# Pacing the gathers of a GNN layer: a gather begins when the last but one has landed, on four semaphores in turn

## The chip, the cores and the metric

The kernel runs on one core of one Trainium2 chip. The metric is the device time in microseconds (us) of one execution, and the median of several such executions. A profiled execution has a span, which is the time from its first to its last instruction on the core, and a device time of its own beside it.

The names in the profile: PE is TensorE (its matmuls), PEld its weight loads, DVE is VectorE, ACT is ScalarE, POOL is GpSimd, SP is SyncE. A `q` behind a name (SPq, ACTq) is the engine's instruction queue, where it issues transfers. L480 is line 480 of the kernel before.

## The reference

One message-passing layer over 12,500 nodes and 412,500 edges, which are sorted by their target:

```python
edge_index = jnp.stack([src, dst])
h = jnp.maximum(_layernorm(x, axis=-1), 0.0)            # x: (12500, 32)
e_feat = jnp.concatenate([h[rol], h[col], edge_attr], axis=-1)   # rol = src, col = dst, 412500 edges
h1 = jax.nn.relu(e_feat @ W1 + b1)                      # W1: (96, 64)
v = h1 @ W2 + b2                                        # W2: (64, 32)
x_cand = jax.ops.segment_max(v, col, num_segments=num_nodes)
x = x + jnp.maximum(x_cand, h)
```

## The kernel before

**Tiles.** The edges are cut into C = 403 chunks of CE = 1024. A chunk's 1024 source rows lie in eight columns of 128. Seven of them (GK = COLS - 1 = 7) are fetched by GpSimd, one indirect DMA for a column: 128 rows of 128 bytes out of `h_rows` in device memory into `feat`. The eighth column is made on chip, by a product of one-hot keys with a table (`select` on TensorE, `take_selected` on VectorE). There are 7 x 403 = 2821 gathers in all.

**Rings.** `feat` has UNROLL = 16 slots, one chunk each, so GpSimd can be up to 16 chunks ahead of TensorE. Each slot has a semaphore of its own, `gathered0` to `gathered15`. A gather adds 16 to it when it has landed, a chunk's seven add TURN = 112. GpSimd waits at every second chunk for `feat_turned`, which says that TensorE has read the slot that is to be filled again; besides, at every eighth chunk, for the indices.

**Steps.** TensorE works in steps of two chunks (202 steps: the last has one chunk). A step v on TensorE holds, in this order: `first_layer(v-1)` (ps_hid, L580 and L582), `turn_ends(v-2)` (ps_turned, L603), `turn_features(v)` (ps_feat, L537: it waits for the gathers, transposes the chunk and raises `feat_turned`), `select` (ps_spare, L570, 14 matmuls), `second_layer(v-1)` (ps_val, L591), `pick_ends(v-2)` (ps_picked, L612), `select` again. VectorE takes each `select`'s result at L958, in the order of its own program, and then the running maximum (L929) that `turn_ends` waits for. ScalarE takes `ps_hid` at L722.

**Loads.** ScalarE's queue issues, at every second step, the target places (L255, 512 KB) and edge attributes (L258, 512 KB) of four chunks. SyncE's queue issues for the same four chunks the term rows (L320, 64 KB each), keys (L336) and keep masks (L326). All orders are written out by hand; nothing is scheduled by a planner.

**Around the loop.** Ahead of the steps stand the layer norm and the terms of each node (`node_terms`, which copies at L296 and L304 what TensorE made); behind them the final maximum.

Of the kernel before, what the change touches and what calls it, by code (L numbers as in the profile page):

```python
# [20 lines left out]
UNROLL = 2 * RING  # L21
TWO = 2
UP = UNROLL // TWO
IDX = 4 * RING
PRE = 5
GK = COLS - 1
SA = 14
SG = 7
ROUND = 1.5 * 2 ** 23
# [6 lines left out]
def gnn_layer(nc, x, src, dst, edge_attr, W1, b1, W2, b2, src_cols, dst_first, attr_rows, sel_rows, sel_cols, out):  # L36
# [23 lines left out]
    REST = N - FULLP * T  # L60
    assert FULLP < P and T == SA * SG
    CPAD = sel_rows.shape[0]
    SN = SA * D

# [9 lines left out]
    def rows_of(b):  # L74
        return min(P, C - b * P)

    ctx = ExitStack()
    with ctx:
        def sb(name, shape, dt=F32):
            return ctx.enter_context(nc.sbuf_tensor(name, shape, dt))  # L80
# [4 lines left out]
        def sem(name):  # L85
            return ctx.enter_context(nc.semaphore(name))
# [21 lines left out]
        key_i = sb("key_i", [P, SG], I32)  # L108
        off_i = sb("off_i", [P, SA], I32)
        off_place = sb("off_place", [P, SA])  # L110

# [72 lines left out]
        s_names = """const_ready root_ready blocks_ready w_in row_pad pads dst_in firsts_in x_win_in  # L184
            cent_done sq_done var_ready std_ready norm_step h_even_done h_stored
            base_step fall_done keep_staged end_staged half_ready end_turned end_kept loc_staged stage_pad zeros_ready term_stored
            chunk_begun feat_turned feat_t_ready edge_hot_ready hid_sum hid_ready val_sum val_ready
            best_half run_ready ends_turned ends_ready ends_split pick_ready best_done best_zero
            check_step worst_ready flag_turned flag_ready
            fin_turned fin_max fin_step out_ready out_done  # L190
# [1 line left out]
            any_in any_gather_begun any_turned any_t_ready any_hid_sum any_hid_ready  # L192
            any_val_sum any_val_ready any_begun any_zero any_done any_all_done"""
        S = {n: sem(n) for n in s_names.split()}
        s_gather = [sem(f"gathered{r}") for r in range(UNROLL)]
        s_idx = [sem(f"idx_in{n}") for n in range(IDX // RING)]
        s_keep = [sem(f"keep_in{n}") for n in range(2)]
        s_key = [sem(f"key_in{n}") for n in range(2)]
# [20 lines left out]
        AUX = 16 * (2 + FOUR)  # L219
        NP, NG = -(-C // TWO), -(-C // FOUR)  # L220
        LOOPS = (NP - PRE) // UP
        TURN = 16 * GK

        def known(s):
            return isinstance(s, int)
# [17 lines left out]
        def wide(i, v):  # L243

            return min(TWO, C - TWO * v) if known(i) else TWO
# [203 lines left out]
        def _(pool):  # L449
# [6 lines left out]
            nc.gpsimd.iota(key_i[:], pattern=[[1, SG]], base=0, channel_multiplier=SG).then_inc(S["const_ready"], 1)  # L456
            nc.gpsimd.iota(off_i[:], pattern=[[1, SA]], base=0, channel_multiplier=0).then_inc(S["const_ready"], 1)

            pool.wait_ge(S["blocks_ready"], 2)
            for a in range(2):  # L460
                for z, row in enumerate((0, 2 * D)):
                    k = 2 * D * z + D * a
# [9 lines left out]
            def step(i, c):  # L472
                slot = c % UNROLL
                if c % RING == 0:
                    pool.wait_ge(s_idx[c // RING % 4], i * 16 + (c // IDX * 16 + 16))
                if c % TWO == 0 and (not known(i) or c >= UNROLL):
                    pool.wait_ge(S["feat_turned"], i * UNROLL + ((c - UNROLL) // TWO + 1))
                pool.sem_inc(S["chunk_begun"], 1)
                for k in range(GK):
                    nc.gpsimd.indirect_dma_start(  # L480
                        feat[:, slot, k, :], None, h_dram,
                        bass.IndirectOffsetOnAxis(ap=idx[:, c % IDX, k:k + 1].bitcast(U32), axis=0),
                    ).then_inc(s_gather[slot], 16)

            begin = UNROLL + (C - UNROLL) % IDX
            for c in range(begin):
                step(0, c)
            with pool.Fori(0, (C - begin) // IDX) as i:
                for u in range(IDX):
                    step(i, begin + u)  # L490
# [25 lines left out]
        def _(pe):  # L516
# [12 lines left out]
            def turn_features(i, v):  # L529
                n = wide(i, v)  # L530
                pe.wait_ge(S["sel_ready"], i * UNROLL + TWO * v + n)
                for c in range(TWO * v, TWO * v + n):
                    slot = c % UNROLL
                    pe.wait_ge(s_gather[slot], i * TURN + (c // UNROLL * TURN + TURN))
                    for b in range(2):
                        to = 2 * P * (c % TWO) + P * b
                        mm = pe.transpose(ps_feat[:, to:to + P],  # L537
                                          feat[:, slot, Q * b:Q * b + Q, :].rearrange("p q d -> p (q d)"), ident[:])
                mm.then_inc(S["feat_turned"], 1)
# [4 lines left out]
            for b in range(NB):  # L544
                r = rows_of(b)
# [71 lines left out]
            def step(i, v):  # L617
                if later(i, v):
                    first_layer(i, v - 1)
                if later(i, v - 1):  # L620
                    turn_ends(i, v - 2)
                turn_features(i, v)
                if is_chunk(i, TWO * v + 2):
                    select(i, TWO * v + 2)
                if later(i, v):
                    second_layer(i, v - 1)
                if later(i, v - 1):
                    pick_ends(i, v - 2)
                if is_chunk(i, TWO * v + 3):
                    select(i, TWO * v + 3)  # L630
# [54 lines left out]
        def _(act):  # L685
            act.wait_ge(S["root_ready"], 1)
            nc.scalar.activation(root_first[:], root_first[:], ACT.Sqrt)
            for n, (a, z) in enumerate(halves):
# [6 lines left out]
            nc.scalar.copy(table[0][:].rearrange("p g (f a) -> p g a f", f=D),  # L695
                           h_even.rearrange("p (g a) f -> p g a f", a=SA)).then_inc(S["table_ready"], 1)
            act.wait_ge(S["base_step"], 3)
# [91 lines left out]
        def _(dve):  # L789
# [164 lines left out]
            def take_selected(i, c):  # L954
                if known(i) and c % TWO:
# [8 lines left out]
                dve.wait_ge(S["sel_step"], i * UNROLL + c + 1)  # L964
                nc.vector.tensor_reduce(feat[:, c % UNROLL, GK, :], sel_tmp[:].rearrange("p (f a) -> p f a", a=SA),  # L965
                                        AX.X, ALU.add).then_inc(S["sel_ready"], 1)
# [142 lines left out]
```

## Time and profile before

| | us |
|---|---|
| median of 3 executions | 4759.94 (4747.39 to 4760.97) |
| the profiled execution, device time | 4765.93 |
| the profiled execution, span | 4764.1 |
| POOL busy (2716.6 of it in 2821 gathers, 963 ns each) | 2733.4 (57%) |
| PE busy | 2960.5 (62%) |
| DVE busy | 2078.8 (44%) |
| ACT busy | 748.1 (16%) |
| mean share of the 16 DMA engines | q10 9.1%, q1 7.4%, q0 (the gathers) 7.1% |
| mean granted clock of TensorE | 0.801 of full speed |

Busy time is time in which an engine executes; a POOL gather counts as busy only while its descriptors are made, not until its rows have landed. The time in which an engine waits is ended by a releaser, which the profile infers: another engine's operation, a DMA, "issue" (nothing that it shows) or "remote" (an update of a semaphore that it can't put to an operation in time).

### The profile page before, as it was taken

To read this page: it belongs to the slowest core of one execution; us is meant where nothing else is said; L and a number is where in the kernel's file an instruction comes from. 1 tells how busy PE (TensorE), PEld (TensorE's weight loads), DVE (VectorE), ACT (ScalarE), POOL (GpSimd) and SP (SyncE) were. 2 spreads that over 40 slices of the span, in tenths; PEclk is the share of its full clock that TensorE was granted. 3 is DMA by queue.
4 is the path that set the end of the run, shared out by engine and by line. 5 is a ranking of instruction groups with operands and counts; after the bars stand their busy time and mean duration, and the time that the engine had idled before them with its cause. 6 is when DMAs were issued, how large, how long until landed. Compare 5 with 4: busy or idle time off the path is not lost.

```text
span 4764.1 us, 41821 instructions
## 1 busy us (share of the span) xinstructions
PE 2960.5 (62%) x11492; PEld 2111.3 (44%) x11492; DVE 2078.8 (44%) x3562; ACT 748.1 (16%) x1058; POOL 2733.4 (57%) x2852
## 2 busy tenths in 40 slices
PE   1266566567676666666666666565766656565677
PEld 0144344445454444444444444444544444444445
DVE  5044344444444444444444444343444434444447
ACT  3011111111111111111111111111111111111111
POOL 6456555556665556565566556555655555565550
PEclk8578778788787878887888887778878888787788
DMA  4322222222222222222222222222222222221222
GB/s 99 76 58 53 46 54 47 52 49 59 49 53 47 56 50 55 50 54 47 53 51 51 54 49 51 51 47 52 55 48 50 47 53 51 49 58 43 53 52 44
DMA packets 245595, 252.33 MB, mean 53 GB/s; under 512 B 83265, under 2 KB 199479, under 8 KB 239113
## 3 DMA queue, kind: packets, MB, share of 16 engines
q10 hardware_dynamic: 20790, 103.55, 9.1%
q1 hardware_dynamic: 133938, 101.54, 7.4%
q0 software_dynamic: 90784, 46.48, 7.1%
q14 instruction: 73, 0.59, 0.0%
q8 instruction: 10, 0.16, 0.0%
HBM read 239.86 MB, written 11.52 MB: 53 GB/s over the span
## 4 chain that ended last, share of the span: by engine, by line
another core or an unknown queue 44%; PE 21%; DVE 15%; issue 14%; DVEq 3%; ACT 3%; ACTq 1%; SPq 0%; DMA 0%; POOL 0%; POOLq 0%
PE ps_spare L570 11%; DVE sel_tmp L958 3%; DVE running L929 3%; DVE best L995 3%; PE ps_turned L603 2%; DVE key_hot L947 2%; DVEq L989 2%; PE ps_hid L582 2%; PE ps_val L591 1%; PE ps_feat L537 1%; PE ps_hid L580 1%; DVE edge_hot L940 1%; PE ps_picked L612 1%; DVE feat L965 1%
## 5 line engine op out<-in xcount | busy, mean ns | idle before, releaser
L480 POOL DMA_INDIRECT feat<-h_rows,idx x2821 | 2716.6, 963 | 1900.3 <-issue 993.3
L570 PE MATMUL ps_spare<-table,key_hot 128*128 128x448 f32 x5642 | 1500.6, 426 | 395.6 <-DVE sel_tmp L958 348.0
L570 PEld LDWEIGHTS ps_spare<-table,key_hot 128*128 128x128 f32 x5642 | 1259.8, 230 | 524.3 <-DVE sel_tmp L958 339.0
L958 DVE SCALAR_TENSOR_TENSOR sel_tmp<-off_place,offset,ps_spare 128x448 f32<-128x448 f32 x403 | 273.6, 679 | 1553.4 <-remote 1234.1
L603 PE MATMUL ps_turned<-ident,running 128*128 128x128 f32 x806 | 171.9, 351 | 939.4 <-DVE running L929 733.7
L722 ACT ACTIVATE hidden<-ps_hid,b_col 128x1024 f32<-128x1024 f32 x202 | 224.8, 1113 | 2681.5 <-remote 2196.6
L603 PEld LDWEIGHTS ps_turned<-ident,running 128*128 128x128 f32 x806 | 116.2, 175 | 1088.5 <-DVE running L929 805.1
L980 DVE TENSOR_TENSOR ends<-ps_turned,ends 128x512 fp32r<-128x512 f32 x202 | 139.5, 690 | 786.4 <-ACT ends L734 579.8
L995 DVE TENSOR_TENSOR best<-ps_picked,best 32x64 f32 x1612 | 355.0, 220 | 162.9 <-remote 96.6
L947 DVE TENSOR_TENSOR key_hot<-dst_rows,ps_iota 128x1792 fp32r<-128x1792 f32 x202 | 406.1, 2011 | 18.1 <-DMA dst_rows<-key_rows 18.1
L580 PE MATMUL ps_hid<-feat_t,w_blk 128*128 128x512 f32 x806 | 413.8, 595 | 0.0
L582 PE MATMUL ps_hid<-edge_hot,term_ring 128*128 128x512 f32 x806 | 411.5, 592 | 0.0
L612 PEld LDWEIGHTS ps_picked<-end_hot,ends 128*128 128x128 f32 x1612 | 238.6, 219 | 296.7 <-issue 157.2
L612 PE MATMUL ps_picked<-end_hot,ends 128*128 128x256 f32 x1612 | 284.1, 326 | 108.5 <-DVE ends L980 63.2
L591 PE MATMUL ps_val<-hidden,w_blk 128*64 128x512 f32 (+1 forms) x808 | 240.5, 676 | 176.8 <-ACT hidden L722 113.3
L741 ACT COPY feat_t<-ps_feat 64x512 f32<-64x512 f32 x404 | 234.3, 580 | 207.0 <-remote 145.1
L965 DVE TENSOR_REDUCE feat<-sel_tmp 128x32 f32<-128x448 f32 x403 | 249.9, 620 | 13.9
L929 DVE TENSOR_TENSOR_SCAN running<-dst_rows,ps_val 128x512 f32<-128x512 bf16 x202 | 243.9, 1207 | 0.0
L971 DVE TENSOR_TENSOR end_hot<-ps_iota,end_all 128x1024 fp32r<-128x1024 f32 x202 | 241.5, 1195 | 0.0
L582 PEld LDWEIGHTS ps_hid<-edge_hot,term_ring 128*128 128x128 f32 x806 | 152.8, 190 | 194.2 <-issue 194.2
L750 ACT ACTIVATE ps_val<-ps_val,b_col 128x512 f32<-128x512 f32 x202 | 133.5, 661 | 614.8 <-PE ps_val L591 304.4
L580 PEld LDWEIGHTS ps_hid<-feat_t,w_blk 128*128 128x128 f32 x806 | 155.5, 193 | 103.5 <-issue 96.2
(125 smaller groups left out, 893.7 us busy)
## 6 DMA issues: line engine op xcount, KB each, us to landing
dst_rows<-loc_rows ACTq DMA_DIRECT2D x98, 512.0 KB
feat_t<-attr_rows_in ACTq DMA_DIRECT2D x98, 512.0 KB
feat<-h_rows,idx POOLq DMA_INDIRECT x2821
dst_rows<-key_rows SPq DMA_DIRECT2D x101, 256.0 KB
term_ring<-term_rows SPq DMA_DIRECT2D x404, 64.0 KB
dst_rows<-keep_rows SPq DMA_DIRECT2D x100, 256.0 KB
term_rows<-best SPq DMA_DIRECT2D x3, 1792.0 KB
idx<-src_cols_in SPq DMA_DIRECT2D x51, 32.0 KB
```

The lines of the kernel that those rows point to most:

```text
L480: nc.gpsimd.indirect_dma_start(feat[:, slot, k, :], None, h_dram, bass.IndirectOffsetOnAxis(ap=idx[:, c % IDX, k:k + 1].bitcast(U32), axis=0),
L570: mm = pe.matmul(ps_sel, key_hot[:, c // TWO % 2, g, P * (c % TWO):P * (c % TWO) + P], table[half][:, g, :], start=(g == 0 and half == 0), ...
L580: pe.matmul(ps_hid[:, c, :], w1_blk[:], feat_t[:, slot, :], start=True, stop=False, skip_group_check=True)
L582: mm = pe.matmul(ps_hid[:, c, :], term_ring[:, slot, :], edge_hot[:, c, :], start=False, stop=True, skip_group_check=True)
L591: mm = pe.matmul(ps_val[HID * r:HID * r + HID, 0:n * 2 * P], w2_blk[:], hidden[:, 0:n, r, :], start=True, stop=True, skip_group_check=True)
L603: mm = pe.transpose(ps_turned[:, to:to + P], running[:, c, b, :], ident[:])
L612: mm = pe.matmul(ps_picked[:, Q * WIN * c:Q * WIN * c + Q * WIN], ends[half][:, c, b, :], end_hot[:, c, Q * b:Q * b + Q, :].rearrange("p q ...
L929: nc.vector.tensor_tensor_scan(running[:, 0:n, :, :].rearrange("p c b n -> p (c b n)"), keep_ring[:, slot:slot + n, :].rearrange("p c n -> ...
L947: nc.vector.tensor_tensor(key_hot[:, v % 2, :, :], key_ring[:, slot:slot + TWO, :].rearrange("p c e -> p (c e)").unsqueeze(1) .broadcast_t ...
L958: nc.vector.scalar_tensor_tensor(out=sel_tmp[:].rearrange("p (f a) -> p f a", a=SA), in0=off_place[:].unsqueeze(1).broadcast_to([P, D, SA] ...
L965: nc.vector.tensor_reduce(feat[:, c % UNROLL, GK, :], sel_tmp[:].rearrange("p (f a) -> p f a", a=SA), AX.X, ALU.add).then_inc(S["sel_ready ...
L995: mm = nc.vector.tensor_tensor(col, ps_picked[D * q:D * q + D, to:to + WIN], col, ALU.max)
```

## The change

Every gather from the third on first waits on GpSimd until the gather two before it has landed, and counts this in a new semaphore `paced`, on which nobody waits. The 16 semaphores of the slots give way to four, which take the gathers in turn: gather number `at` uses `gathered[at % 4]`. TensorE, which waited for a chunk on one semaphore, now waits on all four.

```diff
+LANES = 4
+NEAR = 2
...
-            chunk_begun feat_turned feat_t_ready edge_hot_ready hid_sum hid_ready val_sum val_ready
+            chunk_begun paced feat_turned feat_t_ready edge_hot_ready hid_sum hid_ready val_sum val_ready
...
-        s_gather = [sem(f"gathered{r}") for r in range(UNROLL)]
+        s_gather = [sem(f"gathered{r}") for r in range(LANES)]
...
-        TURN = 16 * GK
+        TURN = 16 // LANES * GK
...
                 for k in range(GK):
+                    at = GK * c + k
+                    if at >= NEAR:
+                        pool.wait_ge(s_gather[(at - NEAR) % LANES],
+                                     i * (IDX * TURN) + 16 * ((at - NEAR) // LANES + 1))
+                        pool.sem_inc(S["paced"], 1)
                     nc.gpsimd.indirect_dma_start(
                         feat[:, slot, k, :], None, h_dram,
                         bass.IndirectOffsetOnAxis(ap=idx[:, c % IDX, k:k + 1].bitcast(U32), axis=0),
-                    ).then_inc(s_gather[slot], 16)
+                    ).then_inc(s_gather[at % LANES], 16)
...
                     slot = c % UNROLL
-                    pe.wait_ge(s_gather[slot], i * TURN + (c // UNROLL * TURN + TURN))
+                    for at in range(GK * c + GK - LANES, GK * c + GK):
+                        pe.wait_ge(s_gather[at % LANES], i * (UNROLL * TURN) + 16 * (at // LANES + 1))
```

On GpSimd (POOL), before, two chunks in the middle of the loop: one wait ahead of 14 gathers (x13 stands for 13 rows alike).

```order
L477 REGISTER_ALU
L480 DMA feat<-h_rows,idx 128x32 [waits feat_turned]
L480 DMA feat<-h_rows,idx 128x32 x13
```

The same place after the change (L487 is the gather, L484 the wait on a lane, L479 the wait for `feat_turned`): the first gathers of two chunks.

```order
L479 ISA
L487 DMA feat<-h_rows,idx 128x32 [waits feat_turned,gathered2]
L487 DMA feat<-h_rows,idx 128x32 [waits gathered3]
L484 REGISTER_ALU
L487 DMA feat<-h_rows,idx 128x32 [waits gathered0]
L487 DMA feat<-h_rows,idx 128x32 [waits gathered1]
L487 DMA feat<-h_rows,idx 128x32 [waits gathered2]
L487 DMA feat<-h_rows,idx 128x32 [waits gathered3]
```

Each gather has a wait of its own now, and at every fourth stands a register operation more, for the value that the next round waits for.

On TensorE (PE), before, `turn_features` of a step near the program's start: a wait on one semaphore for each chunk.

```order
L537 MATMUL ps_feat<-ident,feat 128x128 [waits gathered4,sel_ready]
L537 MATMUL ps_feat<-ident,feat 128x128
L537 MATMUL ps_feat<-ident,feat 128x128 [waits gathered5]
L537 MATMUL ps_feat<-ident,feat 128x128
```

The same rows after the change (L545).

```order
L545 MATMUL ps_feat<-ident,feat 128x128 [waits gathered3,gathered2,gathered0,gathered1,sel_ready]
L545 MATMUL ps_feat<-ident,feat 128x128
L545 MATMUL ps_feat<-ident,feat 128x128 [waits gathered2,gathered3,gathered1,gathered0]
L545 MATMUL ps_feat<-ident,feat 128x128
```

The matmuls are the same and stand in the same order; three waits more stand ahead of each chunk.

## Rows read from the trace of the kernel before

**Rows 1.** The page: the span, the chain that ended last, the gathers' group
```profile
span 4764.1 us, 41821 instructions
...
another core or an unknown queue 44%; PE 21%; DVE 15%; issue 14%; DVEq 3%; ACT 3%; ACTq 1%; SPq 0%; DMA 0%; POOL 0%; POOLq 0%
...
L480 POOL DMA_INDIRECT feat<-h_rows,idx x2821 | 2716.6, 963 | 1900.3 <-issue 993.3
```

**Rows 2.** Windows of the whole run: busy us of each engine (instructions), granted clock, DMA share, GB/s
```profile
0.00:232.00 232.00, 46.10 (x143) 28.86 (x144) 81.09 (x108) 51.23 (x49) 125.95 (x138) 0.69 0.36 88
232.00:4627.00 4395.00, 2803.11 (x10826) 2004.63 (x10825) 1900.08 (x3279) 668.26 (x966) 2599.96 (x2709) 0.80 0.23 51
4627.00:4714.00 87.00, 86.30 (x394) 59.70 (x392) 68.38 (x119) 25.24 (x38) 0.00 (x0) 1.00 0.23 54
4714.00:4764.10 50.10, 25.05 (x136) 18.12 (x132) 29.28 (x57) 3.37 (x7) 7.51 (x5) 0.73 0.21 33
```

**Rows 3.** Waits of POOL: us in total, times, longest
```profile
POOL feat L480 <- PE ps_feat L537: 626.6, 82, 16.4
```

**Rows 4.** Timeline of one step: start us, us, operation [idle before <-releaser]
```profile
2017.32 1.19 POOL L480 DMA_INDIRECT feat<-h_rows,idx  x1 [8.65 <-PE ps_feat L537]
2018.81 0.95 POOL L480 DMA_INDIRECT feat<-h_rows,idx  x1 [0.30 <-issue]
...
2023.07 3.01 PE L570 MATMUL ps_spare<-table,key_hot 128*128 128x448 f32 x14
...
2033.01 0.68 DVE L958 SCALAR_TENSOR_TENSOR sel_tmp<-off_place,offset,ps_spare 128x448 f32<-128x448 f32 x1 [6.62 <-remote]
...
2033.82 0.95 POOL L480 DMA_INDIRECT feat<-h_rows,idx  x1 [0.30 <-issue]
...
2036.43 1.06 PE L537 MATMUL ps_feat<-ident,feat 128*128 128x128 f32 x4
...
2038.28 0.95 POOL L480 DMA_INDIRECT feat<-h_rows,idx  x1 [3.51 <-PE ps_feat L537]
```

**Rows 5.** Timeline of a step behind the last gather
```profile
4629.81 0.60 PE L537 MATMUL ps_feat<-ident,feat 128*128 128x128 f32 x4
...
4635.24 3.05 PE L570 MATMUL ps_spare<-table,key_hot 128*128 128x448 f32 x14
...
4638.56 0.68 DVE L958 SCALAR_TENSOR_TENSOR sel_tmp<-off_place,offset,ps_spare 128x448 f32<-128x448 f32 x1
...
4642.00 0.60 PE L537 MATMUL ps_feat<-ident,feat 128*128 128x128 f32 x4
```

**Rows 6.** Timeline of ACT ahead of the steps (the node terms)
```profile
151.67 0.27 ACT L296 COPY running<-ps_val 128x128 f32<-128x128 f32 x1 [16.26 <-remote]
...
168.47 0.27 ACT L296 COPY running<-ps_val 128x128 f32<-128x128 f32 x1 [16.26 <-remote]
...
198.66 0.27 ACT L296 COPY running<-ps_val 128x128 f32<-128x128 f32 x1 [1.59 <-PE ps_val L526]
```

**Rows 7.** Windows behind a run of gathers, without loads (columns of Rows 2)
```profile
2035.60:2035.80 0.20, 0.20 (x2) 0.20 (x3) 0.20 (x1) 0.00 (x0) 0.00 (x0) 0.50 0.29 36
2035.80:2036.00 0.20, 0.20 (x2) 0.20 (x2) 0.20 (x1) 0.00 (x0) 0.00 (x0) 0.50 0.01 0
```

**Rows 8.** Timeline: two issues of ACT's load, and the last gather ahead of a pause
```profile
1990.67 0.58 ACTq L255 DMA_DIRECT2D dst_rows<-loc_rows  x1
...
2007.72 0.95 POOL L480 DMA_INDIRECT feat<-h_rows,idx  x1 [0.30 <-issue]
...
2037.32 0.58 ACTq L255 DMA_DIRECT2D dst_rows<-loc_rows  x1
```

**Rows 9.** Windows in and behind the stretch of that load (columns of Rows 2)
```profile
2005.00:2007.00 2.00, 0.00 (x0) 0.00 (x0) 0.00 (x0) 0.00 (x0) 1.48 (x2) 0.87 0.19 60
...
2012.00:2013.00 1.00, 0.00 (x0) 0.00 (x0) 0.92 (x2) 0.97 (x1) 0.00 (x0) 0.50 0.12 31
...
2014.00:2016.00 2.00, 1.44 (x7) 1.44 (x8) 1.62 (x2) 0.28 (x1) 0.00 (x0) 0.50 0.00 0
```

## The prediction

> **What bounds the kernel now.** I read the page first, because its chain says whether an engine is the bound. It isn't: 44% of the 4764.1 us, some 2096 us, lie with "another core or an unknown queue", no engine has more than 21%, and the gathers' group has 1900.3 us of idle time before it [rows 1]. So I cut the run into windows [rows 2]. Between 232 and 4627 us GpSimd issues 2709 gathers, 14 to a step, so 193.5 steps take 4395 us: 22.7 us a step and 1.62 us a gather. Behind the last gather, from 4627 to 4714 us, TensorE is busy for 86.30 of 87.00 us, and the step is over in 12.19 us (from L537 at 4629.81 to L537 at 4642.00) [rows 5], though the DMA engines' share is 0.23 in both windows. Loads alone don't slow a step; gathers do.
>
> The timeline of one step shows how [rows 4]. GpSimd is 16 chunks ahead and full; it waits for `feat_turned` (626.6 us of such waits are put to TensorE [rows 3]), then issues 14 gathers, each 0.95 us and 0.30 us behind the one before, 17.5 us in all. L570 ends at 2023.07 + 3.01 = 2026.08, yet VectorE, which waits for it, starts L958 at 2033.01, 6.93 us late. Behind the last gather the same pair is 0.27 us apart (4638.29 to 4638.56) [rows 5]. Ahead of the steps it is the same: ScalarE's copies of TensorE's results come every 16.80 us while gathers run and wait 16.26 us, and wait 1.59 us when they have stopped [rows 6]. So TensorE's results are announced late while gathers run in a row, GpSimd then pauses, since it is full, and the pause lets them through. A step is 17.5 us of gathers and a pause, 8.65 and 3.51 us in these rows.
>
> **The change part by part.** The loads, the matmuls and the gathers stay. What moves is when a gather starts. Its start becomes the landing of the gather two before it, plus the time from a semaphore to a gather's start. That time is now hidden, since the queue is fed ahead, except at a burst's start: L537 ends at 2036.43 + 1.06 = 2037.49, and the gather starts at 2038.28, 0.79 us later [rows 4]. It contains a wait and an increment already, so `paced` is costed at nothing more; if every wait cost another 0.30 us, the gap between gathers, each gather would.
>
> *Landing, quiet.* No row shows a landing. The last gather of a burst starts at 2033.82, and the share of the DMA engines is 0.29 until 2035.8 and 0.01 after [rows 4, 7]: 2.0 us. A gather that starts behind a wait takes up to 1.19 instead of 0.95 us [rows 4]. I take 2.2. Two gathers to 2.2 + 0.79 us is 1.50 us each, against 1.25.
>
> *Landing beside the loads.* ScalarE's load comes every 2037.32 - 1990.67 = 46.65 us, for four chunks, 28 gathers [rows 8], and its engines are busy until the window of 2014, so for some 23 us [rows 9]. The landing there is 2.2 at least and, since the gather of 2007.72 had surely landed by 2014.0, 6.3 us at most. I take 3.5, nearer to the low end, because the engines' mean share is only 0.19 there [rows 9] and two gathers are under way instead of 6.3 / 1.25 = 5. That is (3.5 + 0.79) / 2 = 2.15 us a gather.
>
> *Sum.* Of 28 gathers 23 / 2.15 = 10.7 begin beside the loads, the other 17.3 take 17.3 x 1.50 = 26 us: 49 us for four chunks, against 45.4 now. GpSimd becomes the bound: 24.5 us for 14 gathers. Under it lie TensorE's 12.19 us a step and even its late announcements. The first 112 gathers fill the ring by 30 + 112 x 1.50 = 198 us, ahead of the 232 us at which the first slot is free again. Then 2709 / 28 = 96.75 groups x 48.95 = 4736 us, and behind them a landing of 2.2 and the 50.1 us of the last window [rows 2], as TensorE is no longer behind: 232 + 4736 + 52 = 5020 us of span. The profiled execution's own time is 1.8 us above its span and 6.0 above the median: 5016 us, 5.4% slower.
>
> TensorE's three waits more for each chunk, six a step, have no row; at the 0.30 us of a GpSimd gap they are 1.8 us a step. I take nothing: TensorE would have 24.5 us for 12.19. If GpSimd weren't the bound, they could cost 193.5 x 1.8 = 350 us.
>
> The notes on the chip speak of the same landing. The Trainium skill, "DMA: Bandwidth & Descriptors", in "Anatomy of one DMA — SWDGE (gpsimd) path", gives a DMA from GpSimd a fixed 2.0 us, mostly the receipt of the last write, plus bytes / 436e3: an estimate of 2.04 us for 16 KB. The quiet windows agree (2.0 us). By that figure for all gathers, also beside loads, the interval would be 1.42 us and the sum 4127 us.
>
> **The rivals.** *Faster: the landing stays short beside the loads.* The same sum with 1.50 us for all 2709 gathers is 232 + 4064 + 52 = 4348 of span, 4344 us. For it speak the low share of the engines and the prompt step behind the last gather [rows 5, 9]. Against it: loads of 1 MB are issued at once, and the burst's last gather may take 6.3 us. It decides at one number: four chunks must take under (4764 - 284) / 96.75 = 46.3 us, so 12.5 gathers must fit in 23 us, 1.84 us each, a landing of 2.89 us. The fixed cost that the Trainium skill states as constant is this case. The same page, in "Queues, rings and completion order", says that each DMA engine takes turns between its queues a packet at a time, which would lengthen it; no row here separates the queues. Chance 0.21.
>
> *Much slower.* Either the landing beside loads is near 6.3 us: 3.55 us a gather, 6.5 in 23 us and 21.5 x 1.50 = 32.3 behind: 55.3 us for four chunks, 5630 us. Or the slower flow still holds back TensorE's announcements until GpSimd pauses: a step is then 24.5 us and a pause of 3.51, 28.0, and 193.5 x 28.0 + 284 - 4 = 5698 us. Ahead of the steps the gathers did it without the steps' loads [rows 6]; no row shows them at 1.50 us. Chance 0.24.
>
> *Nothing changes.* If the queue hides the 0.79 us, a landing of 2.2 us is over before the gather two later would start anyway (2.5 us), and beside loads 1.75 us a gather still gives 13.1 in 23 us and 14.9 x 1.25 = 18.6 behind, 41.6 in all, under the 45.4 of now. The steps and their pauses stay: 4760 us. Against it stands that the wait comes ahead of the issue, where the 0.79 us was measured. Chance 0.07.
>
> **How the numbers follow.** The forecast, 4800 to 5250 us, has 0.48. A measurement of this kernel tells about 0.3% from no change, 14 us. Faster: 0.21 and a little of the third: 0.22. Within: 0.05. Slower: 0.73. For 8 in 10 I leave out the ends of both rivals, a tenth at each side: 4480 to 5560; the forecast's own range is 4800 to 5250, for landings beside loads of 3.0 to 4.4 us and 0.03 us more or less in quiet time.
>
> **What the profile would show.** Right: GpSimd's gathers mostly wait on a DMA or "remote" and not on TensorE; their starts lie 1.5 us apart in quiet time and about 2 beside loads; the wait for `feat_turned` is gone; TensorE's idle time is ended by gathers at `turn_features`; the end comes some 52 us behind the last gather. L958 follows L570 within a microsecond more often than now. Wrong: intervals under 1.65 us on the mean (faster), or waits for `feat_turned` that stay beside late L958s (the announcements are still held back). I'd be wrong above all by the landing beside loads, which no row gives.

## The result, and the profile after

The changed kernel takes 6042.69 us (median of 4 executions, 6032.24 to 6050.42), the kernel before beside it 4753.66 (4 executions, 4707.94 to 4760.97): a ratio of 1.274, interval 1.265 to 1.282. It is slower, as forecast, but by 27% and not by 5.4%, and it lies outside the range. The profiled execution took 6032.24 us.

The page of the changed kernel: its span, the chain that ended last, and the groups of the gathers and of `turn_features`.

```profile
span 6030.4 us, 46408 instructions
...
DMA 60%; issue 26%; POOL 12%; POOLq 1%; DVE 1%; PE 0%; DVEq 0%; SPq 0%; ACT 0%
...
L487 POOL DMA_INDIRECT feat<-h_rows,idx x2821 | 2701.2, 958 | 3269.4 <-DMA feat<-h_rows,idx 2342.8
L545 PE MATMUL ps_feat<-ident,feat 128*128 128x128 f32 x806 | 211.2, 355 | 2992.7 <-DMA feat<-h_rows,idx 2991.1
```

Before, 44% of the chain lay with "another core or an unknown queue" [rows 1]. Now 60% is the landing of gathers and 12% their making. A gather is still made in 958 ns; the idle time before gathers has grown from 1900.3 us [rows 1] to 3269.4, and landings end most of it (2342.8 us). TensorE waits for gathers, 2991.1 us in all.

The waits of the changed kernel: us in total, times, longest.

```profile
DVE sel_tmp L966 <- PE ps_spare L578: 3474.1, 199, 25.5
...
PE ps_feat L545 <- DMA feat<-h_rows,idx: 2991.1, 220, 22.6
...
POOL feat L487 <- DMA feat<-h_rows,idx: 2342.8, 1192, 7.4
...
POOL feat L487 <- issue: 907.3, 1628, 7.3
```

No wait of GpSimd is put to TensorE any more (626.6 us before [rows 3]): its ring is never full. VectorE's wait at L966 is now ended by TensorE itself; none of its waits ends in "remote", as this one did before:

```profile
DVE sel_tmp L958 <- remote: 1234.1, 156, 27.8
```

GpSimd's timeline around one load of ScalarE in the changed kernel.

```profile
3022.41 0.95 POOL L487 DMA_INDIRECT feat<-h_rows,idx  x1 [1.40 <-DMA feat<-h_rows,idx]
3023.66 0.95 POOL L487 DMA_INDIRECT feat<-h_rows,idx  x1 [0.30 <-issue]
3025.49 1.32 POOL L487 DMA_INDIRECT feat<-h_rows,idx  x1 [0.89 <-issue]
3031.30 0.95 POOL L487 DMA_INDIRECT feat<-h_rows,idx  x1 [4.48 <-DMA feat<-h_rows,idx]
3033.17 0.95 POOL L487 DMA_INDIRECT feat<-h_rows,idx  x1 [0.93 <-DMA feat<-h_rows,idx]
3037.30 0.95 POOL L487 DMA_INDIRECT feat<-h_rows,idx  x1 [3.18 <-DMA feat<-h_rows,idx]
3038.98 0.95 POOL L487 DMA_INDIRECT feat<-h_rows,idx  x1 [0.73 <-DMA feat<-h_rows,idx]
3044.31 0.95 POOL L487 DMA_INDIRECT feat<-h_rows,idx  x1 [4.38 <-DMA feat<-h_rows,idx]
...
3056.81 0.95 POOL L487 DMA_INDIRECT feat<-h_rows,idx  x1 [0.85 <-DMA feat<-h_rows,idx]
...
3063.09 0.95 POOL L487 DMA_INDIRECT feat<-h_rows,idx  x1 [4.01 <-DMA feat<-h_rows,idx]
3064.34 0.95 POOL L487 DMA_INDIRECT feat<-h_rows,idx  x1 [0.30 <-issue]
3066.31 0.95 POOL L487 DMA_INDIRECT feat<-h_rows,idx  x1 [1.03 <-DMA feat<-h_rows,idx]
3067.57 0.95 POOL L487 DMA_INDIRECT feat<-h_rows,idx  x1 [0.30 <-issue]
3069.53 0.95 POOL L487 DMA_INDIRECT feat<-h_rows,idx  x1 [1.02 <-DMA feat<-h_rows,idx]
```

From its timeline of all engines: one `select` and VectorE behind it, and the issues of loads.

```profile
3016.78 3.05 PE L578 MATMUL ps_spare<-table,key_hot 128*128 128x448 f32 x14
...
3020.10 0.68 DVE L966 SCALAR_TENSOR_TENSOR sel_tmp<-off_place,offset,ps_spare 128x448 f32<-128x448 f32 x1
...
3023.44 0.58 ACTq L257 DMA_DIRECT2D dst_rows<-loc_rows  x1
...
3056.67 0.59 SPq L328 DMA_DIRECT2D dst_rows<-keep_rows  x1
```

If a gather starts 0.79 us [rows 4] behind the landing of the one two before it, starts give landings (the time from a gather's start to its landing). Quiet: 3069.53 - 0.79 - 3066.31 = 2.43 us, and a pair every 3.22 us, 1.61 us a gather. Beside the load: 3031.30 - 0.79 - 3023.66 = 6.85 us, 3037.30 - 0.79 - 3031.30 = 5.21, 3044.31 - 0.79 - 3037.30 = 6.22, and for the gather of 3033.17, which is waited for by that of 3038.98, 5.02: 5.0 to 6.9 us. Seven intervals take 3044.31 - 3022.41 = 21.9 us, 3.13 us a gather. A second disturbance of 5.49 us (3063.09 - 0.79 - 3056.81) stands beside SyncE's load of keep masks at 3056.67. L578 ends at 3019.83, and L966 starts 0.27 us later, so this result is prompt; that of rows 4 was taken 6.93 us late.

This stretch isn't a rare one. Between 1500 and 4500 us the trace has 51 whole rounds of four chunks from one issue of ScalarE's load to the next, 58.8 us each. On the mean the gathers that start within 21 us of the issue take 22.1 us for 6.9 intervals, 10.9 us more than 6.9 x 1.61; the other 21 of a round take 2.8 us more than at 1.61. SyncE issues its four term rows in the same 21 us (in the round of 3023.44 from 3024.41 to 3041.09).

The same windows of the changed kernel: first behind the load's issue, then the remainder of its stretch, then a quiet one (columns of Rows 2).

```profile
3027.00:3029.00 2.00, 0.00 (x0) 0.00 (x0) 0.00 (x0) 0.00 (x0) 0.00 (x0) 0.52 0.91 203
3029.00:3042.00 13.00, 0.00 (x0) 0.00 (x0) 0.00 (x0) 0.00 (x0) 3.78 (x4) 0.50 0.16 50
3048.00:3057.00 9.00, 9.00 (x39) 5.67 (x38) 7.84 (x15) 0.66 (x1) 5.34 (x7) 1.00 0.06 11
```

Gathers land late also where the engines' mean share is 0.16, the same as 2.6 of 16 engines busy all the time. In the quiet stretch TensorE is busy all 9.00 us; in the 15 us of the load it doesn't run at all.

### The profile page after: what moved, and what is told of

It reads as the page before. It is cut to its first block, busy times and chain, and to the rows that moved or that the text cites. A ratio compares the mean times of both kernels' runs of the same rounds, so it can differ in the third digit from the quotient of the medians.

```text
span 6030.4 us, 46408 instructions
## 1 busy us (share of the span) xinstructions
PE 2907.4 (48%) x11492; PEld 2084.2 (35%) x11492; DVE 2079.2 (34%) x3562; ACT 750.1 (12%) x1058; POOL 2718.0 (45%) x2852
## 4 chain that ended last, share of the span: by engine, by line
DMA 60%; issue 26%; POOL 12%; POOLq 1%; DVE 1%; PE 0%; DVEq 0%; SPq 0%; ACT 0%
DMA feat<-h_rows,idx 60%; POOL feat L487 12%; POOLq L486 0%; POOLq L484 0%; DVE feat L1078 0%; POOLq L480 0%; PE ps_spare L578 0%; PE ps_picked L620 0%; POOLq L479 0%; DVE best L809 0%; DVE best L1003 0%; DMA h_rows<-best 0%; DVE best L819 0%; DVE var L825 0%; DVE mean L814 0%
## 5 line engine op out<-in xcount | busy, mean ns | idle before, releaser
L487 POOL DMA_INDIRECT feat<-h_rows,idx x2821 | 2701.2, 958 | 3269.4 <-DMA feat<-h_rows,idx 2342.8
L545 PE MATMUL ps_feat<-ident,feat 128*128 128x128 f32 x806 | 211.2, 355 | 2992.7 <-DMA feat<-h_rows,idx 2991.1
L578 PE MATMUL ps_spare<-table,key_hot 128*128 128x448 f32 x5642 | 1571.3, 441 | 32.5 <-DVE key_hot L955 24.3
L966 DVE SCALAR_TENSOR_TENSOR sel_tmp<-off_place,offset,ps_spare 128x448 f32<-128x448 f32 x403 | 274.2, 681 | 3538.3 <-PE ps_spare L578 3474.1
L578 PEld LDWEIGHTS ps_spare<-table,key_hot 128*128 128x128 f32 x5642 | 1321.0, 241 | 161.2 <-issue 34.4
L545 PEld LDWEIGHTS ps_feat<-ident,feat 128*128 128x128 f32 x806 | 107.9, 173 | 3041.2 <-issue 2995.2
L730 ACT ACTIVATE hidden<-ps_hid,b_col 128x1024 f32<-128x1024 f32 x202 | 224.7, 1112 | 1369.7 <-PE ps_hid L590 1261.5
L620 PEld LDWEIGHTS ps_picked<-end_hot,ends 128*128 128x128 f32 x1612 | 203.9, 189 | 165.1 <-issue 161.5
L620 PE MATMUL ps_picked<-end_hot,ends 128*128 128x256 f32 x1612 | 245.5, 295 | 1.9 <-DVE ends L988 1.9
L599 PE MATMUL ps_val<-hidden,w_blk 128*64 128x512 f32 (+1 forms) x808 | 218.4, 619 | 0.0
```

The lines of the kernel that those rows point to most:

```text
L487: nc.gpsimd.indirect_dma_start(feat[:, slot, k, :], None, h_dram, bass.IndirectOffsetOnAxis(ap=idx[:, c % IDX, k:k + 1].bitcast(U32), axis=0),
L545: mm = pe.transpose(ps_feat[:, to:to + P], feat[:, slot, Q * b:Q * b + Q, :].rearrange("p q d -> p (q d)"), ident[:])
L578: mm = pe.matmul(ps_sel, key_hot[:, c // TWO % 2, g, P * (c % TWO):P * (c % TWO) + P], table[half][:, g, :], start=(g == 0 and half == 0), ...
L620: mm = pe.matmul(ps_picked[:, Q * WIN * c:Q * WIN * c + Q * WIN], ends[half][:, c, b, :], end_hot[:, c, Q * b:Q * b + Q, :].rearrange("p q ...
L966: nc.vector.scalar_tensor_tensor(out=sel_tmp[:].rearrange("p (f a) -> p f a", a=SA), in0=off_place[:].unsqueeze(1).broadcast_to([P, D, SA] ...
```

## The experiments

Where a group of runs has no interval below, the runs of the kernel before beside it spread by 3.7%, and their lowest and highest are given instead.

### How many gathers may be under way, and what the waits cost

`free16` has `LANES = 16, NEAR = 16`, `near3` and `near4` have `LANES = 4` and `NEAR = 3` or `4`:

```diff
-LANES = 4
-NEAR = 2
+LANES = 4
+NEAR = 4
```

(and on TensorE the loop over lanes starts at `GK * c + GK - min(LANES, GK)`). `small_loads` is the changed kernel, with ScalarE's loads cut down from the ninth chunk on (the edit is shortened here); the computation then uses old rows, so this kernel serves for its time alone:

```diff
-            eng.dma_start(loc_ring[:, lo:hi, :].rearrange("p c e -> p (c e)"),
-                          loc_dram[:, bass.ds(s, count), :] ...
+            eng.dma_start(loc_ring[0:1, lo:hi, :].rearrange("p c e -> p (c e)"),
+                          loc_dram[0:1, bass.ds(s, count), :] ...
-            eng.dma_start(feat_t[2 * D:P, lo:hi, :] ...
+            eng.dma_start(feat_t[2 * D:2 * D + 1, lo:hi, :] ...
```

> The changed kernel with sixteen semaphores in turn and the wait on the gather sixteen before: every wait, count and register operation of the change is still there, but that gather has long landed. Theory A (the pace is the landing of the gather two before, plus the time from its semaphore to a start, divided by two): nothing binds any more, GpSimd's gathers lie 1.25 to 1.35 us apart again with pauses for feat_turned, and the time is that of the kernel before, 4700 to 4800 us. Rival B (the waits, the counting and the split over several semaphores cost the time themselves, on GpSimd or on TensorE): it stays near the changed kernel, 5500 to 6050 us.

> The changed kernel waits on the gather three before (four semaphores as before). Theory A with a landing that doesn't depend on how many gathers are under way (2.4 us quiet, 5.9 beside the loads): quiet gathers at GpSimd's own 1.25 to 1.3 us, beside the loads (5.9 + 0.8) / 3 = 2.2 us, so 10 in 23 us and 18 x 1.28 = 23: 46 us for four chunks, 4740 us in all, or 4800 with the keys' and masks' stretch. Rival C (beside the loads the two DMA engines that they keep busy let through only so many gathers, whatever is under way): the gathers there stay 3.3 us apart, about 54 us for four chunks, 5500 us. Rival B: near 6040 us.

> The changed kernel waits on the gather four before. Theory A: quiet 1.25 to 1.3 us, beside the loads (5.9 + 0.8) / 4 = 1.7 us, 13.5 in 23 us and 14.5 x 1.28 = 18.6: 42 us for four chunks, under the 45.4 of the kernel before, so GpSimd fills its ring, pauses for feat_turned again and TensorE's late announcements set the step: 4700 to 4800 us. Rival C: 3.3 us a gather beside the loads, about 5500 us. Rival B: near 6040 us.

> The changed kernel, but from the ninth chunk on ScalarE's two loads of four chunks carry only one partition each, of the target places and of the edge attributes; the computation then uses old ones. Theory A: the long landings are due to these loads, so nearly all gathers take 1.6 us: 28 x 1.6 = 45 us for four chunks, 4350 + 284 = 4630 us, up to 4800 with what the keys, masks and term rows still do. Rival B, or if the long landings come from SyncE's loads or from the gathers themselves: above 5600 us.

| kernel | us, median (range) |
|---|---|
| before, same chip | 4835.82 (4706.28 to 4882.06) |
| free16 | 5116.45 (5094.36 to 5149.54) |
| near3 | 4979.82 (4962.36 to 4990.38) |
| near4 | 4569.44 (4539.59 to 4613.91) |
| small_loads | 5236.60 (5226.87 to 5245.84) |

The wait for a near landing makes the time of the changed kernel: 6043 with two gathers under way, 4980 with three, 4569 with four, at the same number of instructions. Rival B falls as an explanation of the 6043, and rival C (a fixed rate beside the loads, 5500 us for three and for four) with it. But theory A's numbers failed. For free16, with waits that never bind, it had the time of the kernel before, and free16 stands over 200 us above the slowest run of it. near3 is some 180 us above its 4800. And near4 is under its 4700, and below every run of before. In all three results of TensorE are late; the sums left this out, or had the wrong size for it. The waits of free16, and then of near4:

```profile
ACT hidden L730 <- remote: 3020.6, 190, 19.1
DVE sel_tmp L966 <- remote: 1846.6, 181, 24.1
...
POOL feat L487 <- PE ps_feat L545: 1232.5, 153, 22.9
```

```profile
ACT hidden L730 <- remote: 1066.4, 31, 63.5
...
DVE sel_tmp L966 <- remote: 801.1, 95, 42.3
POOL feat L487 <- DMA feat<-h_rows,idx: 656.0, 679, 4.0
```

In free16, results are late at nearly every step (190 times at L730), and GpSimd stands with a full ring for 1232.5 us, against 626.6 before [rows 3]. In near4 TensorE's results are late seldom and then for long (31 times at L730, up to 63.5 us). That it catches up in the stretches in which GpSimd waits for landings was seen in one place of the trace and not counted.

`small_loads` gives 806 us of the changed kernel to ScalarE's two loads, under two thirds of the 1240 us and more that were expected; the last section of the experiments finds the rest.

### The pace of the gathers against the wait for a landing

The kernel before, with one, two or three small additions on GpSimd ahead of each gather; of `fill2`, which has two, the lines at the gather:

```diff
+                    nc.gpsimd.tensor_tensor(out=spare[:, at % 2, 0:4], in0=ident[:, 0:4], in1=ident[:, 0:4], op=ALU.add).then_inc(S["filled"], 1)
+                    nc.gpsimd.tensor_tensor(out=spare[:, at % 2, 4:8], in0=ident[:, 0:4], in1=ident[:, 0:4], op=ALU.add).then_inc(S["filled"], 1)
+                    if at > 0:
+                        pool.wait_ge(S["filled"], i * (IDX * GK * 2) + at * 2)
+                        pool.sem_inc(S["paced"], 1)
```

The wait is for the additions ahead of the gather before, long done.

> The kernel before with one small addition (128x4) on GpSimd ahead of each gather, which waits for nothing but the addition before it; landings are not waited for. Gathers are spread from 1.25 to some 1.35 to 1.4 us. Theory E (TensorE's results are announced late when gathers follow each other too fast, whatever is in flight): fewer late ones than before, a step of 14 x 1.4 = 19.6 us and a shorter pause, 4300 to 4750 us. Rival F (they are late as long as landings are not waited for): the pause of 5.2 us stays, 24.8 us a step, 5080 us.

> The same with three such additions ahead of each gather: some 1.5 to 1.7 us a gather, the quiet pace of the changed kernel, but with landings not waited for. Theory E: results are announced within 0.5 us nearly always, no pause for feat_turned, GpSimd's pace alone sets the time: 193.5 steps x 14 x 1.6 = 4334, + 284 = 4620 us (4350 to 4890 for 1.5 to 1.7 us). Rival F: the results stay late by several us, a step is 22.4 + 5.2 = 27.6 us, 5600 us.

> The kernel before with two additions ahead of each gather, between fill1 (1.34 us a gather, results still late) and fill3 (1.63 us, none late). Theory E, and the point from which results are late lies below 1.48: 1.48 us for each of 2821 gathers, 30 + 4175 + 55 = 4260 us. If it lies above 1.48, late results and pauses as in fill1: 20.7 + 4 us a step, 4780 to 5060 us.

| kernel | us from gather to gather in a row | us, median (range) | before, same chip |
|---|---|---|---|
| fill1 | 1.34 | 4864.19 (4810.92 to 4908.09) | 4833.36 (4727.96 to 4904.86) |
| fill2 | 1.48 | 4338.64 (4336.19 to 4339.68) | 4740.09, ratio 0.916 (0.913 to 0.919) |
| fill3 | 1.63 | 4752.39 (4748.19 to 4754.61) | 4833.36 (4727.96 to 4904.86) |

The page of fill3, its span and its chain, and then from its waits that of VectorE at L967, which is L958 of the kernel before:

```profile
span 4746.3 us, 55793 instructions
...
POOL 66%; issue 30%; POOLq 1%; DVE 1%; PE 0%; DMA 0%; DVEq 0%; SPq 0%; ACT 0%
```

```profile
DVE sel_tmp L967 <- PE ps_spare L579: 1973.2, 183, 14.9
```

The timeline of GpSimd in fill3, three gathers of one kind:

```profile
2399.06 0.96 POOL L489 DMA_INDIRECT feat<-h_rows,idx  x1 [0.15 <-POOL spare L485]
...
2400.68 0.96 POOL L489 DMA_INDIRECT feat<-h_rows,idx  x1 [0.15 <-POOL spare L485]
...
2402.31 0.96 POOL L489 DMA_INDIRECT feat<-h_rows,idx  x1
```

At fill3's and fill2's pace theory E holds. At 1.63 us a gather and no landing waited for, the chain is GpSimd with its issues, no wait of VectorE or ScalarE ends in "remote", and no stretch of the loads is seen in the pace. The 4752 us are about the changed kernel's quiet pace all through; the changed kernel's other 1290 us (on another chip) go to waiting on landings beside loads. In fill2 some waits still end late, at L966 these:

```profile
DVE sel_tmp L966 <- remote: 241.6, 90, 7.9
```

But no wait of its GpSimd is put to TensorE, so the ring is never full and they don't set the step. fill1 came out by neither theory: 4864 us is above the 4750 of theory E and under the 5080 of rival F, and its GpSimd waits 731.2 us with a full ring. fill2 beats the kernel before on its chip by 8.4%. Its time is 28% under the changed kernel's on another chip.

### Where late results come from: waits, increments, and the chip

`far_slots` is the kernel before (one semaphore a slot, one wait a chunk on TensorE), with a wait that never binds and the count:

```diff
+                    if c >= 2:
+                        pool.wait_ge(s_gather[(c - 2) % UNROLL],
+                                     i * (IDX // UNROLL * TURN) + (c - 2) // UNROLL * TURN + TURN)
+                        pool.sem_inc(S["paced"], 1)
```

`counted` has the increment alone. `told4` is near4 with one wait on TensorE, on the count (the last four gathers are counted behind the loop):

```diff
-                    for at in range(GK * c + GK - min(LANES, GK), GK * c + GK):
-                        pe.wait_ge(s_gather[at % LANES], i * (UNROLL * TURN) + 16 * (at // LANES + 1))
+                    pe.wait_ge(S["paced"], i * (UNROLL * GK) + GK * c + GK)
```

> The kernel before, with its sixteen semaphores of the slots and one wait a chunk on TensorE, but every gather waits on GpSimd for the chunk two before (14 to 8 gathers back, landed long ago) and counts this in paced. It is the GpSimd side of free16 without the gathers dealt out over lanes. Theory A2 (the 350 us that free16 stood above the kernel before come from TensorE, which had seven waits for a chunk instead of one): this one is at the kernel before, within 1.5%, 4700 to 4880 us. Rival B2 (they come from GpSimd's waits and counting): it is near free16, 5050 to 5150 us.

> near4 (four semaphores in turn, each gather waits for the one four before), but TensorE waits for a chunk only once, on the count paced that GpSimd raises as it finds each gather landed; the last four are counted behind the loop. Theory A2 (waits on TensorE cost when GpSimd doesn't bind): a little under near4's 4569 us, some 4400 to 4550, as three waits a chunk fall away where free16's six more cost 350 us. Rival B2: no difference, 4540 to 4610 us; or slower, up to 4750, as a chunk is known four gathers later.

> The kernel before with one increment of a semaphore ahead of each gather on GpSimd, and no wait. far_slots, with wait and increment, came out 350 to 500 us above the kernel before. Theory J (the increment itself costs, as one more update beside each gather): 5050 to 5250 us. Rival K (the wait does it): 4700 to 4880 us.

`fill12` has one and two additions in turn ahead of the gathers:

> The kernel before with one and two additions ahead of gathers in turn: 1.34 and 1.48 us, 1.41 on the mean, between fill1 (results late, 4864 us) and fill2 (prompt, 4339 us). If TensorE's results are announced promptly down to 1.41 us: 30 + 2821 x 1.42 + 55 = 4090 us. If they are late: 19.8 us of gathers a step and a pause of some 4 us, 4700 to 4900 us.

far_slots took 5245.23 us (5239.33 to 5258.62), over 300 us above the slowest run of before beside it, with one wait a chunk on TensorE. So theory A2 fell: the cost comes without more waits on TensorE. told4 doesn't decide it: its 4535.29 us (4502.51 to 4610.63) lie in theory A2's range and 5 us under rival B2's, and its runs overlap near4's, which ran on another chip. Then came a chip on which the kernel before took 3649.94 us (13 executions, 3648.20 to 3653.21), counted 3649.57 (ratio 1.000, 0.999 to 1.001) and fill12 4135.53 (ratio 1.134, 1.132 to 1.135). Rows of counted there, around L959 (L958 before):

```profile
2028.72 3.05 PE L571 MATMUL ps_spare<-table,key_hot 128*128 128x448 f32 x14
...
2032.04 0.68 DVE L959 SCALAR_TENSOR_TENSOR sel_tmp<-off_place,offset,ps_spare 128x448 f32<-128x448 f32 x1
```

L571 ends at 2031.77 and L959 starts 0.27 us later, with gathers 1.25 us apart all the while. On this chip no wait is ended by "remote", GpSimd's 2821 x 1.25 = 3526 us and what stands around them set the time, and adding to them only costs. The three were run again on another chip:

> counted again. On the chip of the last runs the kernel before took 3650 us with no result of TensorE late, so counted (3650 us too) said nothing of what the increment does where they are late. If this chip shows late results (before at 4700 to 4880 us): theory J (the increment makes them later) 5050 to 5250 us, rival K (the wait does) 4700 to 4880 us. If it doesn't, 3650 us by either.

> far_slots again, beside counted and the kernel before on one chip. Where results are late: 5200 to 5300 us, as before. Where they aren't: waits that never bind cost nothing and it is at the kernel before, 3650 us; if it is over 3750 us there, a wait costs GpSimd time of its own.

> fill12 again (1.41 us a gather on the mean). Where results are late in the kernel before: 4135 us, as on the last chip, if they come promptly at this pace, 4700 to 4900 us if not. Where they aren't late: 4135 us.

There before took 4757.11 us (13 executions), counted_b 4950.94 (ratio 1.044, 1.037 to 1.051), far_slots_b 5030.24 (1.058, 1.052 to 1.065) and fill12_b 4729.65 (0.995, 0.990 to 0.999). The timeline of counted_b, the same kernel as counted:

```profile
2023.12 3.01 PE L571 MATMUL ps_spare<-table,key_hot 128*128 128x448 f32 x14
...
2038.54 0.68 DVE L959 SCALAR_TENSOR_TENSOR sel_tmp<-off_place,offset,ps_spare 128x448 f32<-128x448 f32 x1 [6.37 <-remote]
```

L571 ends at 2026.13, and VectorE takes its result 12.41 us later, having waited idle for the last 6.37 us. Where results are late, one more increment beside each gather makes the kernel 4.4% slower, and wait and increment together 5.8%: theory J for most of it, though both times are under the ranges that were expected (5050 to 5250 and 5200 to 5300 us). Both ratios are smaller than what the first chips suggested (far_slots there 5245 against 4833 us). The pace at which late results stop setting the step lies between fill12's 1.41 us on the mean and fill2's 1.48, on the chips that have them; the two were run on different ones, so that a difference of chips isn't excluded. The additions bring increments of their own, two to three a gather, so the pace alone may be allowed to be faster than that.

### What makes landings long beside the loads

`spread_after` loads the same target places, as two transfers:

```diff
-            eng.dma_start(loc_ring[:, lo:hi, :].rearrange("p c e -> p (c e)"),
-                          loc_dram[:, bass.ds(s, count), :].rearrange("r c e -> r (c e)").unsqueeze(1)
-                          .broadcast_to([2, WIN, count * ANY])).then_inc(s_aux[half], 16)
+            for r in range(2):
+                eng.dma_start(loc_ring[WIN * r:WIN * r + WIN, lo:hi, :].rearrange("p c e -> p (c e)"),
+                              loc_dram[r, bass.ds(s, count), :].rearrange("c e -> (c e)").unsqueeze(0)
+                              .broadcast_to([WIN, count * ANY])).then_inc(s_aux[half], 16)
```

`small_attr` cuts the edge attributes' load alone; `small_all` cuts, beside ScalarE's two, SyncE's keys, masks and term rows (both compute with old rows); `told4_spread` is told4 with the two transfers.

> The changed kernel, the same bytes loaded, but the load of the target places is issued as two transfers of 64 partitions instead of one whose outer dimension is two. Theory G (landings are long beside the loads because that load runs on two or three of the 16 DMA engines for some 20 us, and each gather has rows on those): the load is spread over the engines and over in a few us, and most of the 806 us that small_loads gained come back without leaving anything out: 5200 to 5450 us. Rival H (it is the bytes, or the number of transfers, in whatever shape): near the changed kernel, 5950 to 6150 us.

> The changed kernel, but of ScalarE's two loads only that of the edge attributes carries one partition (old ones are used); that of the target places is whole. small_loads took 806 us off the changed kernel, both loads together. Theory G (the target places' load on a few engines makes most of the long landings): little is gained, 5750 to 6000 us, and the target places keep 500 us or more. Rival H (the bytes count, and both loads have as many): half, near 5640 us.

> As small_loads (of the target places and edge attributes one partition each from the ninth chunk on), and of the keys, keep masks and term rows one partition each too; the computation uses old ones. Theory A: what is left is the quiet pace of waiting for the gather two before, 1.60 us for each of 2821 gathers: 29 + 4512 + 50 = 4590 us, up to 4700. If it stays above 4900, landings are also long without any load beside them.

> told4 with the target places' load in two transfers of 64 partitions. With shorter landings beside the loads the gathers run nearer to 1.25 us there. Theory G with E: less waiting on landings, but more time with gathers in a row and late results: between 4400 and 4750 us, near told4's 4535. Theory G alone: 4250 to 4450 us.

| kernel | us, median (range) | loads whole |
|---|---|---|
| the changed kernel | 6042.69 (6032.24 to 6050.42) | all |
| small_attr | 5851.89 (5844.09 to 5863.89) | all but edge attributes |
| spread_after | 5641.23 (5628.01 to 5650.71) | all, target places in two transfers |
| small_loads | 5236.60 (5226.87 to 5245.84) | SyncE's |
| small_all | 4685.94 (4684.28 to 4687.73) | the indices alone |

These ran on several chips. The changed kernel's ring is never full and its results are prompt, so the difference between chips above shouldn't touch it. small_attr bears this out in part: on the chip on which the kernel before takes 3650 us, every other gather of a quiet stretch starts at 2461.00, 2464.17, 2467.24 and 2470.34, 3.1 to 3.2 us a pair as in the changed kernel. The changed kernel itself ran on one chip only.

Taken away in this order, the edge attributes make 191 us, the target places with the same number of bytes 615, SyncE's loads 551. What is left, 4686 us less some 80 at both ends, is 1.63 us a gather. The order matters: SyncE's term rows are issued in the same stretch as ScalarE's loads, and no run leaves out SyncE's alone. But it isn't the bytes: 512 KB of edge attributes cost 191 us, 512 KB of target places 615. Loading these as two transfers gave back 401 us. That is between the ranges of theory G (5200 to 5450 us) and rival H (5950 to 6150): the load's shape counts, and it isn't all. Windows of spread_after behind an issue at 2444.04 (columns of Rows 2):

```profile
2446.00:2448.00 2.00, 0.00 (x0) 0.00 (x0) 1.35 (x2) 0.44 (x1) 1.40 (x2) 0.98 1.11 245
2448.00:2450.00 2.00, 0.00 (x0) 0.00 (x0) 0.00 (x0) 0.00 (x0) 0.64 (x1) 0.50 0.89 203
2450.00:2452.00 2.00, 0.00 (x0) 0.00 (x0) 0.00 (x0) 0.00 (x0) 0.00 (x0) 0.50 0.26 49
...
2456.00:2458.00 2.00, 0.00 (x0) 0.00 (x0) 0.00 (x0) 0.00 (x0) 0.28 (x1) 0.50 0.15 36
2458.00:2462.00 4.00, 0.39 (x3) 0.42 (x3) 0.00 (x0) 0.00 (x0) 1.89 (x2) 0.50 0.03 4
```

and its gathers in the same stretch:

```profile
2446.30 0.95 POOL L488 DMA_INDIRECT feat<-h_rows,idx  x1 [2.35 <-DMA feat<-h_rows,idx]
2447.55 1.10 POOL L488 DMA_INDIRECT feat<-h_rows,idx  x1 [0.30 <-issue]
2453.93 0.95 POOL L488 DMA_INDIRECT feat<-h_rows,idx  x1 [5.28 <-DMA feat<-h_rows,idx]
2455.33 0.95 POOL L488 DMA_INDIRECT feat<-h_rows,idx  x1 [0.46 <-issue]
2459.12 0.95 POOL L488 DMA_INDIRECT feat<-h_rows,idx  x1 [2.84 <-DMA feat<-h_rows,idx]
2460.37 0.95 POOL L488 DMA_INDIRECT feat<-h_rows,idx  x1 [0.30 <-issue]
2462.25 0.95 POOL L488 DMA_INDIRECT feat<-h_rows,idx  x1 [0.93 <-DMA feat<-h_rows,idx]
```

The first landing is as long as before (2453.93 - 0.79 - 2446.30 = 6.84 us), the later ones are shorter (2459.12 - 0.79 - 2453.93 = 4.40 us, against 5.21 and 6.22), and the stretch is over by 2460 us, 16 us behind the issue and not 21. From 2450 to 2458 us the share is low here too, 0.15 at the end, and gathers still land late; which transfers these are, no run says. These are the rows of one stretch, and others of this trace have single landings above 7 us.

told4_spread took 4853.25 us (4846.21 to 4902.29), ratio 1.024 (1.021 to 1.028) to before on its chip, where told4 took 4535 on another: shorter landings bring gathers in a row back, and with them a full ring (889.7 us of GpSimd's waits are put to TensorE, against 55.6 in told4). Theory G with E had this, up to 4750 us; the measured time is 100 us beyond. That it would be a gain without late results is not shown.

## Why the prediction was right and where it was wrong

**Right: what bounds it.** GpSimd's pace, set by the landing of the gather two before it and 0.79 us from semaphore to start, took the place of the pauses; TensorE waits for gathers, `feat_turned` isn't waited for, no wait ends in "remote", and the end comes 6030.4 - 5979.77 = 50.6 us behind the last gather (52 forecast). The rival in which the announcements stay late at the slower pace didn't happen at two gathers under way; it did at three and four.

**Wrong: the landing beside the loads.** "I take 3.5, nearer to the low end" is the step that failed, and the reasons given for it, a low mean share of the engines and only two gathers under way, don't hold. It was 5.0 to 6.9 us in the stretch above, in part above the 6.3 us that I had put as its upper bound. Of the rivals, that of a landing near 6.3 us has the mechanism that came; its 5630 us are 413 too few. Runs size the term: all loads together cost the changed kernel 6043 - 4686 = 1357 us, and the forecast had 5016 - 4344 = 672 for them. The trace divides them: 10.9 us a round within the 21 us behind ScalarE's issue, where the forecast had 23 - 10.7 x 1.50 = 7.0, and 2.8 us in the rest of the round, where it had nothing. For 98 rounds that is 1068 and 274 us, 1342 of the 1357. So most of this error is the landing beside the loads, and the smaller part a term put at nothing: stretches such as that beside SyncE's keep masks, which the sum took as quiet. The runs that leave loads out give SyncE's 551 of the 1357, but its term rows lie in the first stretch.

**Wrong in size: the quiet pace.** The sum had 2.2 + 0.79 = 3.0 us for two gathers. The trace has 3.22 and small_all 3.27 on the mean: 4686 us where the same sum had 4344, 342 us too few. The two errors, 685 and 342 us, make up the miss of 1027, as they must: small_all's time divides it in two. By the fixed cost of the Trainium skill, "DMA: Bandwidth & Descriptors", "Anatomy of one DMA — SWDGE (gpsimd) path", the estimate was 2.04 us a landing and 4127 us in all. The quiet landing of 2.43 us is not far from it; those of 5.0 to 6.9 us beside the loads are, and there the measurement decides.

**Not tested by the result: the costs put at nothing for `paced` and for TensorE's waits.** In the changed kernel itself `paced` can't be told from the landing that it waits for. In a kernel that TensorE's late results bound they aren't free: 4.4% for the increment, 5.8% with the wait. The 350 us that I put against TensorE's own waits, were GpSimd not the bound, is of the size seen in free16, but far_slots stands as far above the kernel before with one wait a chunk on TensorE. What TensorE's waits cost by themselves stays open: told4 has a quarter of near4's and its median lies 0.7% under it, on another chip.

**Right, and more than the prediction knew: why there was anything to gain.** The pauses of the kernel before were due to late results of TensorE while gathers run in a row. Slowing the gathers from 1.25 to 1.48 us without waiting for a landing gains 8.4% (fill2). And they depend on the chip: on one, counted had none, and the kernel before took 3650 us there.

## What to carry to other kernels

A throttle that waits for a landing needs enough transfers under way: a landing of 2.4 us became 5 to 7 us beside the loads, and two gathers under way leave nothing to cover it, where four did (near4, below every run of before). fill2's, which waits for no landing, gained most. Where a latency is to become a kernel's pace, read its longest values beside every load in the loop, each queue's apart; a mean share of the DMA engines didn't tell it here. And a kernel whose bound is results announced late should be measured on more than one chip before it is tuned against that: fill2 gains 8.4% where they are late, and fill12, which slows the gathers less, loses 13% where they aren't.

## What the runs showed of the hardware that wasn't expected

- The same kernel took 3650 us on one chip and 4700 to 4910 us on at least four others. On the one, TensorE's results are seen 0.27 us behind its last matmul, with gathers from GpSimd every 1.25 us; on another VectorE stood idle 6.37 us for one that had ended 12.41 us before.
- Where they are late, a semaphore increment beside each gather on GpSimd makes it worse (ratio 1.044), where they aren't, it costs nothing (1.000).
- A gather's landing, 2.43 us in quiet, was 5.0 to 6.9 us beside loads, most of that time at a mean share of 0.16. With the target places in two transfers it was 6.84 us at first and 4.40 us later.
- Three additions of 128x4 on GpSimd, with their wait and count, slow its gathers by 0.38 us, 0.09 us for the first and 0.14 to 0.15 for each more.

Open: what holds TensorE's results back while GpSimd makes gathers, and why one chip is free of it. No run here separates it further than the pace and the increments.
